# All chunks written out, dense rows on four row groups, and the last column block ended on VectorE

## What is computed

```python
def _cin_layer(x0, xi, W):                     # W: (64 * Fi, 128)
    Wr = W.reshape(F0_, Fi, Fn)
    return jnp.einsum('bid,bjd,ijn->bnd', x0, xi, Wr)

e = jnp.stack([tbl_0[ids[:, 0]], ...], axis=1)  # 512 samples, 64 fields, 16 numbers
h = x = e
for W in (W0, W1, W2):
    h = _cin_layer(x, h, W)                    # 512, 128, 16
    outs.append(h)
z = jnp.sum(jnp.concatenate(outs, axis=1), axis=-1)         # 512, 384
h = jnp.concatenate([z, dense_ctx], axis=1)                 # 512, 400
h = jnp.maximum(h @ W_top1 + b_top1, 0.0)                   # 512, 512
h = jnp.maximum(h @ W_top2 + b_top2, 0.0)                   # 512, 256
y = h @ W_top3                                              # 512, 1
```

## Time and profile before

| what | value |
|---|---|
| median of 3 runs | 1162.77 us (1161.48 to 1163.68) |
| profiled execution, its own time | 1162.44 us |
| its span, first to last instruction | 1160.6 us |
| TensorE matmuls, busy | 1112.0 us (96%) |
| VectorE, busy | 914.2 us (79%) |
| GpSimd, busy | 889.5 us (77%) |
| ScalarE, busy | 682.6 us (59%) |
| granted TensorE clock, mean | 0.987 |

### The profile page before, as it was taken

One profiled execution on the slowest core, in us unless ns is written; L12 is line 12 of the kernel. 1 busy time (PEld: TensorE's weight loads), 2 busy tenths in 40 slices (PEclk: granted clock), 3 DMA queues, 4 the chain that ended last, 5 costly groups with the idle time before them and its releaser, 6 DMA issues.

```text
span 1160.6 us, 21047 instructions
## 1 busy us (share of the span) xinstructions
PE 1112.0 (96%) x4802; PEld 821.0 (71%) x4802; DVE 914.2 (79%) x2563; ACT 682.6 (59%) x2132; POOL 889.5 (77%) x724
## 2 busy tenths in 40 slices
PE   2998999999999899999999899999999999999999
PEld 2675767777678677777678677777767877776765
DVE  2888888898977688888897678989897689888820
ACT  2354666666654566576674366766665466666731
POOL 6787898989885697898887588898989579856740
PEclk9999999999999899999999999999999999999989
DMA  7583434151536125243442434324253621523000
GB/s 260 141 200 74 106 69 101 21 130 34 125 85 164 42 45 114 60 92 81 92 112 63 112 82 88 81 40 115 36 120 81 165 75 17 136 60 121 1 0 1
DMA packets 127945, 102.78 MB, mean 89 GB/s; under 512 B 77473, under 2 KB 86881, under 8 KB 127298
## 3 DMA queue, kind: packets, MB, share of 16 engines
q1 hardware_dynamic: 117522, 92.79, 32.1%
q0 software_dynamic: 8192, 2.11, 2.2%
q10 hardware_dynamic: 2096, 6.40, 1.4%
HBM read 97.06 MB, written 4.20 MB: 87 GB/s over the span
## 4 chain that ended last, share of the span: by engine, by line
PE 77%; POOL 10%; issue 5%; DVE 3%; DMA 2%; ACT 1%; SPq 0%; DVEq 0%; POOLq 0%; ACTq 0%
PE tps L864 18%; PE tps L866 17%; PE tps L865 17%; PE acc L822 8%; PE side L891 5%; POOL rows_sb L431 3%; PE side L878 3%; PE acc L811 2%; PE acc L806 2%; PE acc L807 2%; DVE parts_sb L578 2%; POOL ysum_sb L447 1%; POOL ysum_sb L451 1%; POOL rows_sb L497 1%; PE acc L817 1%
## 5 line engine op out<-in xcount | busy, mean ns | idle before, releaser
L682 ACT ACTIVATE y_sb<-tps,xcol_sb 128x128 f32<-128x128 f32 x1792 | 510.1, 375 | 381.8 <-PE tps L866 348.4
L578 DVE SCALAR_TENSOR_TENSOR parts_sb<-tps,xcol_sb,parts_sb 128x128 f32<-128x128 f32 x2176 | 606.3, 343 | 156.0 <-PE tps L866 153.5
L864 PE MATMUL tps<-w_hi_sb,h_hi_sb 128*128 128x512 f32 x1024 | 465.8, 455 | 15.7 <-issue 5.4
L866 PE MATMUL tps<-w_hi_sb,h_lo_sb 128*128 128x512 f32 x1024 | 406.6, 397 | 2.7 <-issue 2.7
L865 PE MATMUL tps<-w_lo_sb,h_hi_sb 128*128 128x512 f32 x1024 | 405.6, 396 | 0.0
L431 POOL DMA_INDIRECT rows_sb<-tables,rows_now_sb x240 | 248.8, 1037 | 69.6 <-issue 40.8
L864 PEld LDWEIGHTS tps<-w_hi_sb,h_hi_sb 128*128 128x128 f32 x1024 | 193.4, 189 | 112.8 <-issue 32.1
L865 PEld LDWEIGHTS tps<-w_lo_sb,h_hi_sb 128*128 128x128 f32 x1024 | 193.7, 189 | 64.6 <-issue 28.8
L866 PEld LDWEIGHTS tps<-w_hi_sb,h_lo_sb 128*128 128x128 f32 x1024 | 193.4, 189 | 49.5 <-issue 3.5
L447 POOL TENSOR_TENSOR ysum_sb<-y_sb 128x1024 f32<-128x1024 f32 x64 | 156.9, 2452 | 86.7 <-ACT y_sb L682 85.3
L451 POOL TENSOR_TENSOR ysum_sb<-ysum_sb,y_sb 128x1024 f32<-128x1024 f32 x64 | 160.3, 2505 | 31.5 <-ACT y_sb L682 29.7
(11 more groups left out here) (70 smaller groups left out, 697.5 us busy)
## 6 DMA issues: line engine op xcount, KB each, us to landing
roll_sb<-x_scratch SPq DMA_DIRECT2D x240, 256.0 KB, 4.0
w_sb<-w_rows SPq DMA_DIRECT2D x40, 256.0 KB, 3.7
gsum_sb<-w_rows ACTq DMA_DIRECT2D x8, 512.0 KB, 9.6
roll_sb<-x_halves SPq DMA_DIRECT2D x32, 128.0 KB, 2.9
rows_sb<-tables,rows_now_sb POOLq DMA_INDIRECT x240
x_scratch<-rows_sb SPq DMA_DIRECT2D x30, 128.0 KB, 4.0
xx_sb<-x_scratch SPq DMA_DIRECT2D x15, 256.0 KB, 2.7
roll_sb<-x_scratch SPq DMA_DIRECT2D x30, 64.0 KB, 1.9
```

Of the source, the lines that this page charges most:

```text
L578: dve.scalar_tensor_tensor(part, bank, scale, part, ALU.mult, ALU.add).then_inc(d_done, 1)
L682: done = act.activation(y[:, bank, u * NF:(u + 1) * NF], tps[:, p % RING, u * NF:(u + 1) * NF], ACT.Copy, scale=xcol[:, (q + 1) % 2, s, i: ...
L864: pe.matmul(bank, h1_hi[:, par, cols], w1_hi[:, of], start=True, stop=False, skip_group_check=True)
L866: pe.matmul(bank, h1_lo[:, par, cols], w1_hi[:, of], start=False, stop=True, skip_group_check=True).then_inc(t_ready, 1)
```

## The change

Three edits. The loop is gone: `each_chunk` runs over all 16 chunks in Python, so each engine's program is one straight line, with constants in its waits and addresses. The 16 dense rows and their weights are loaded four times, to partitions 0, 32, 64 and 96, and the four matmuls of `add_part(m, 3)` each read their own copy. In the last column block of chunk 15, GpSimd stops after L453, and the four adds behind it stand at the end of VectorE's program.

```diff
-        dense = top[0:DENSE, 3072:3072 + BATCH]
+        dense = [top[32 * m:32 * m + DENSE, 3072:3072 + BATCH] for m in range(4)]
+        wt1_dense = [wt1[32 * m:32 * m + DENSE, 3, 0:P] for m in range(4)]
...
+        last_step = sem("last_step")
...
-        def each_chunk(eng, chunk):
-            chunk(0, -1, 0)
-            with eng.Fori(0, BLOCKS - 1) as bt:
-                for q in range(PER_BLOCK):
-                    chunk(bt, q, bt * PER_BLOCK + (q + 1))
-            for q in range(PER_BLOCK - 1):
-                chunk(BLOCKS - 1, q, (BLOCKS - 1) * PER_BLOCK + q + 1)
+        def each_chunk(chunk):
+            for t in range(CHUNKS):
+                chunk((t - 1) // PER_BLOCK if t else 0, (t - 1) % PER_BLOCK if t else -1, t)
...
-                            (wt1[0:DENSE, 3, :], ins["W_top1"][3 * P:3 * P + DENSE, :]),
+                            *((wt1_dense[m], ins["W_top1"][3 * P:3 * P + DENSE, m * P:(m + 1) * P]) for m in range(4)),
...
-                            (bt2, ins["b_top2_cols"]), (dense, ins["dense_rows"]),
+                            (bt2, ins["b_top2_cols"]), *((rows_in, ins["dense_rows"]) for rows_in in dense),
...
-                if bank == 6:
+                if bank == 6 and not (is_last(t) and s == SUB - 1):
...
-            each_chunk(pool, chunk)
-            finish_block(PER_BLOCK - 2, CHUNKS - 1, SUB - 1)
+            each_chunk(chunk)
...
-            each_chunk(dve, chunk)
+            each_chunk(chunk)
+
+            last = SUB - 1
+            dve.wait_ge(a_done, CHUNKS * N_A)
+            dve.wait_ge(y_step, ((CHUNKS - 1) * SUB + last) * STEPS_OF_SUM + 3)
+            dve.tensor_tensor(ysum[:, 0:CH], ysum[:, 0:CH], y[:, BLOCK_A - 1], ALU.add).then_inc(last_step, 1)
+            dve.wait_ge(last_step, 1)
+            dve.tensor_tensor(ysum[:, 0:CH // 2], ysum[:, 0:CH // 2], ysum[:, CH // 2:CH], ALU.add).then_inc(last_step, 1)
+            dve.wait_ge(last_step, 2)
+            dve.wait_ge(d_done, CHUNKS * QUAD * N_D)
+            dve.tensor_tensor(ysum[:, 0:CH // 2], ysum[:, 0:CH // 2], parts[:, last % 2].rearrange("p u n -> p (u n)"),
+                              ALU.add).then_inc(last_step, 1)
+            dve.wait_ge(last_step, 3)
+            dve.tensor_tensor(h2t[:, (CHUNKS - 1) % 2, last, :], ysum[:, 0:NF], ysum[:, NF:2 * NF], ALU.add).then_inc(h2t_ready, 1)
...
-            act.wait_ge(top_loaded, 16 * 7)
+            act.wait_ge(top_loaded, 16 * 13)
...
             def add_part(m, part):
-                rows_in = slice(0, DENSE if part == 3 else P)
-                return pe.matmul(tps[:, m, :], wt1[rows_in, part, m * P:(m + 1) * P], dense if part == 3 else z[:, part, :],
+                if part == 3:
+
+                    return pe.matmul(tps[:, m, :], wt1_dense[m], dense[m], start=False, stop=False, skip_group_check=True)
+                return pe.matmul(tps[:, m, :], wt1[:, part, m * P:(m + 1) * P], z[:, part, :],
                                  start=part == 0, stop=part == 2, skip_group_check=True)
...
-            pe.wait_ge(top_loaded, 16 * 7)
+            pe.wait_ge(top_loaded, 16 * 13)
```

More of the change, by code:

```diff
@@ L409, in chunk @@
                             (wt1[:, 0:3, :], ins["W_top1"][0:3 * P, :].rearrange("(k p) n -> p k n", p=P)),
-                            (wt1[0:DENSE, 3, :], ins["W_top1"][3 * P:3 * P + DENSE, :]),
+                            *((wt1_dense[m], ins["W_top1"][3 * P:3 * P + DENSE, m * P:(m + 1) * P]) for m in range(4)),
                             (wt2, ins["W_top2"].rearrange("(k p) n -> p k n", p=P)),
                             (wt3, ins["w_top3_cols"]), (bt1, ins["b_top1_cols"]),
-                            (bt2, ins["b_top2_cols"]), (dense, ins["dense_rows"]),
+                            (bt2, ins["b_top2_cols"]), *((rows_in, ins["dense_rows"]) for rows_in in dense),
                         ):
                             sp.dma_start(dst, src).then_inc(top_loaded, 16)
-            each_chunk(sp, chunk)
+            each_chunk(chunk)
             sp.wait_ge(hid_copied, 7)
@@ L766, in chunk @@
                         scale_bank(q, t, p)
-            each_chunk(act, chunk)
+            each_chunk(chunk)
             for use in range(2):
@@ L950, in chunk @@
                     fill_bank(q, t, p)
-            each_chunk(pe, chunk)
+            each_chunk(chunk)
             def add_part(m, part):
-                rows_in = slice(0, DENSE if part == 3 else P)
-                return pe.matmul(tps[:, m, :], wt1[rows_in, part, m * P:(m + 1) * P], dense if part == 3 else z[:, part, :],
+                if part == 3:
+                    return pe.matmul(tps[:, m, :], wt1_dense[m], dense[m], start=False, stop=False, skip_group_check=True)
+                return pe.matmul(tps[:, m, :], wt1[:, part, m * P:(m + 1) * P], z[:, part, :],
                                  start=part == 0, stop=part == 2, skip_group_check=True)
             form_g(PER_BLOCK - 1, CHUNKS - 1, 0)
-            pe.wait_ge(top_loaded, 16 * 7)
+            pe.wait_ge(top_loaded, 16 * 13)
             pe.wait_ge(z1_summed, CHUNKS)
```

## The result

The changed kernel took 1145.9 us (median of 3 runs, 1145.88 to 1146.3) where the kernel before took 1162.77: a ratio of 0.9857 (0.9835 to 0.9879). The forecast was 1145.6.

The account below looks back on a forecast made before the run. TensorE sets the pace, busy 63.20 us of 63.85 in an undisturbed chunk. From 1162.44 us, 10.9 for the loop and 5.9 for the end come off, giving 1145.6 us; range 1142.5 to 1150.5.

Parts of the forecast that it names:

- the loop: Chunks 1 to 12: removing the jumps back and the register work before waits gains 10.9 us.
- the end: Last chunk: the moved adds, split dense rows and a shorter low-clock stretch together gain 5.9 us.
- The returns: Two jumps back, behind chunks 4 and 8: engines stop for lack of instructions; excess over like chunks sums to 10.86 us.
- Chunk 6's 0.81: Chunk 6: its 64.66 us against 63.85 was counted as excess of the first return, a gain of 0.81 us.
- The register work: Loop chunks: on VectorE, GpSimd and ScalarE, covered by TensorE's work, so worth nothing; at most 2.4 us more over nine chunks.
- a chunk other than the first and those with a contraction takes over 65 us: Chunk windows after the change: a sign named in advance that would show the forecast wrong.
- VectorE's adds: Last column block of chunk 15: four adds take 1.82 us on VectorE, and `form_g` starts 1.33 us sooner.
- The dense rows: Between `form_g` and `sum_h2`: four row groups take two rounds, about 0.9 us; `sum_h2` then waits for ScalarE's copies.
- The clock: Behind the dense rows: half speed lasts about 3.3 us instead of 10.1, losing 1.7 of 7.60 us, so 5.9 gained.
- The end gave all it should: Against the first rival: row groups run serially or the long dip comes, end gains 3.1 to 4.2, 1148 us; 11%.
- the excess did not belong to the block's end: Against the second rival: the returns' excess is block-end work, or the stall stays, so straight code keeps it, 1156.5 us; 5%.
- no code that was reached for the first time stopped TensorE: Against the third rival: new code in chunks 5 to 12 stalls at 5.4 us each, up to 1189 us; 4%.

Follow-up runs that it names:

- e1: The kernel before with its loop written out and nothing else changed; 1151.77 us, ratio 0.9906.
- e3: The changed kernel with chunks 1 to 12 in three loops of one pass each, so no jump back is taken; 1147.13 us, ratio 0.9869.
- e2: The changed kernel with the loop put back, leaving the dense rows' four row groups and VectorE's four adds; 1156.34 us, ratio 0.9945.
- e8: The kernel before with 100 semaphore increments put ahead of TensorE's work, so its loop starts elsewhere in the code; 1158.27 us, ratio 0.997.
- e4: The changed kernel with a loop of two passes over chunks 5 to 12, returning once behind chunk 8; 1147.28 us, ratio 0.9867.
- e11: e9 with the first two gathers of chunk 6 moved to place 52 of chunk 5; 1131.46 us, ratio 0.9736.
- e9: The changed kernel with VectorE's last subtract one place earlier in all chunks but 5 and 9; 1136.06 us, ratio 0.9776.
- e7: The changed kernel with VectorE's last subtract one place earlier in every chunk; 1138.0 us, ratio 0.9787.
- e5: The changed kernel with the dense rows loaded once and their four matmuls on one row group again; 1148.83 us, ratio 0.9883.
- e6: The changed kernel with the last four adds given back to GpSimd; 1146.75 us, ratio 0.9863.

## Why the prediction was right, and where it was not

**The total.** That it came within 0.3 us is luck: the loop gave 0.75 us less than forecast and the end 0.48 more, and within the loop's term larger errors cancelled.

**The returns.** Right in mechanism, as far as the jump goes. With the jumps gone the excess went (e1), with a loop that doesn't jump back it stayed away (e3), and with the loop put back it returned (e2). That what is missing behind the jump is instructions is argued: e8, where the place of the code decides on the second stop, speaks for it, but no trace shows a fetch. The sum, 10.15 measured for 10.9 forecast, is nearer than its parts. Forecast was a gain of 2.51, 2.92, 0.81, 2.48 and 2.14 for chunks 4, 5, 6, 8 and 9. Measured were 2.65, 4.06, a loss of 1.83, then 2.62 and 3.24. Three sizes were off:

- Chunk 6's 0.81 was booked under the first return. By e4 it belongs to GpSimd's stop ahead of the 130th gather, which stays whether there is a loop or not (e11 moved it, and the excess with it).
- Chunks 5 and 9 were measured against a steady chunk of 63.85. That chunk has idle time of its own, from the subtract that collides with GpSimd's add; behind a chunk with a contraction the two miss each other, and 62.71 is due. This hid 1.1 us at each.
- The register work was set at nothing on the ground that it is on VectorE, GpSimd and ScalarE and that TensorE's work covers it, with a gain as the bound. It is on TensorE too (840 ALU operations in the trace of the kernel before). The bound was read from chunk 13, which comes behind a contraction; chunk 14, just as straight, takes 63.92 in the same trace. The register work's removal came out as a small loss: with it gone, the six steady chunks are 0.14 us longer each, 0.8 in all, and chunk 6 is 1.8 longer. e4 shows the first within one kernel, and chunk 6 at 64.68 in loop code; e3, whose loops have lost their register work, has 63.96 and 66.61. For the steady chunks the subtract's 3.25 us for 2.96 says how: another phase of VectorE against GpSimd. In chunk 6 TensorE's wait is 2.18 us for 1.65, and then the subtract takes 3.33 for 1.35 and TensorE stands 0.82 behind it. In e3 and the repeat of the changed kernel a dip of 3.4 us stands there in place of that collision, and the chunk is as long. Why the first wait is longer in straight code wasn't settled.

So "a chunk other than the first and those with a contraction takes over 65 us" did come true, in chunk 6. I had written that this would prove me wrong; it proved one term wrong, and errors of opposite sign, 2.2 us too little for chunks 5 and 9 against 2.6 too much for chunk 6 and 0.8 for the steady ones, cancelled for the most part. The expectation for e4 failed for a related reason: I had taken the 5.9 us of the second return as the price of any, while the second stop and the low clock behind it are in that price only where the code lies so (e4, e8).

**VectorE's adds.** `form_g` forecast 1.33 us sooner within the last chunk, measured 1.51 (55.73 us behind the chunk's start before, 54.22 after). The handovers were smaller than taken, and `add_part` became the bound as foreseen.

**The dense rows.** Forecast two rounds, 0.9 us, and `sum_h2` set by ScalarE; measured 1.14 and so it is. From `form_g` to `sum_h2` it takes 1108.63 - 1105.50 = 3.13 us, forecast 3.12.

**The clock.** Forecast a dip as short as the shortest seen, measured 3.4 us. The first 64 records of the contraction ended 6.37 us sooner for 5.9 (67.28 us behind the chunk's start for 73.65). This was the guess with least behind it: across the runs of this study the dip at the end lasted 0 (e9, e11), 3.4, 6.8, 10.2 and 13.7 us (e8), and e9's last chunk without it took 91.17, 1.62 less than with the short one.

**The rivals.** The end gave all it should; the excess did not belong to the block's end (e3); no code that was reached for the first time stopped TensorE behind the first chunk. One engine did stop for more than 2 us, which I had named as a sign against the forecast: GpSimd, but at the same two gathers in every version, the looped ones too.

## What to carry to other kernels

Read the price of a loop's return from like chunks of the trace, and don't take it for a constant: TensorE stood for 1.9 to 2.4 us each time, and the second stop with the dip behind it, some 3 us more (chunk 5 at 66.77 for 63.23 in e8, chunk 9 at 65.99 for 63.11 in e4), came and went with the place of the code. A chunk without disturbance is no clean measure as long as it has idle time of its own; compare busy with length first, and don't take busy for the floor (63.2 us of it became 62.63 in e7). Once a stall is gone look at what the engines now meet: here the next two gains, some 10 us for one place in a list (e9) and 2.5 in chunk 6 for two gathers issued earlier (e11), lay in a collision and a stop that the first profile held already.

## What the runs showed that I had not expected

- GpSimd stops for 2.0 to 2.2 us between its 129th and 130th indirect gather, and again between the 241st and 242nd, in looped and straight code alike; with both gathers issued earlier the first stop moves along (e11).
- TensorE's second stop behind a jump vanished with 100 more instructions ahead of the loop (e8).
- Eight records of 16 rows on four row groups take 1.14 us, four at a time, against 4.27 in e5, where the clock fell during them.
- The first chunk varies from 73.95 (e1) to 76.89 us (e6) between kernels whose difference lies behind it or is the loop alone, and takes 74.11 and 75.08 in the two traces of the changed kernel. It blurs differences of a microsecond or two in a single profile, so the chunks' own windows are the better measure.
